# A two-layer decoder kernel: query projections in three half-width passes, and probability rings of six places

## The reference, cut to what matters

```python
x = _layernorm(x + _L0_attn_ref(x, ...))        # 16 heads of 8, causal, rope
x = _layernorm(x + _L0_xattn_ref(x, ctx, ...))  # one head of 128 over 1601 rows
x = _layernorm(x + _L0_ffn_ref(x, ...))         # 32 experts, 8 chosen, and a shared one
x = _layernorm(x + _L1_attn_ref(x, ...))        # 16 heads of 8, causal, relative positions
x = _layernorm(x + _L1_xattn_ref(x, ctx, mask, ...))  # 12 heads of 64 over 1601 rows
x = _layernorm(x + _L1_ffn_ref(x, ...))
# in _L1_xattn_ref
q = (query @ Wq.T + bq).reshape(b, tq, H, DH)
k = (cross @ Wk.T + bk).reshape(b, tc, H, DH)
scores = jnp.einsum('bqhd,bkhd->bhqk', q, k) / jnp.sqrt(jnp.float32(DH))
attn = jax.nn.softmax(where(mask, -inf, scores), axis=-1)
```

## Time and profile before

| | us |
|---|---|
| median of 3 runs | 2157.14 |
| lowest and highest of them | 2140.36, 2173.19 |
| the profiled execution's own time | 2159.29 |
| its span, first to last instruction | 2157.5 |
| TensorE busy | 1857.2 (86%) |
| GpSimd busy | 1100.0 (51%) |
| mean granted TensorE clock | 0.906 of full speed |

### The profile page before, as it was taken

The page is one execution under the profiler, slowest core; times in us unless marked ns, Lnnn a source line. Parts: engine busy times, 40 slices in busy tenths (PEclk is TensorE's granted clock), DMA queues, the critical chain, the costliest instruction groups (busy, mean ns, idle before and its releaser), DMA issues.

```text
span 2157.5 us, 50937 instructions
## 1 busy us (share of the span) xinstructions
PE 1857.2 (86%) x19672; PEld 1395.8 (65%) x19672; DVE 1189.9 (55%) x3159; ACT 903.4 (42%) x1875; POOL 1100.0 (51%) x1664
## 2 busy tenths in 40 slices
PE   5666889898898988889898988989888998989996
PEld 3443467576676666666675776756666666767775
DVE  5253447554665546744575546744477545754552
ACT  2522344444443444345343444434443453434443
POOL 2502363557535573356635674354743566356664
PEclk9975689899998998988998999988999899999998
DMA  6000010001000010000100010000000000000000
GB/s 173 26 1 1 1 26 1 1 2 27 4 2 2 2 27 4 1 3 4 27 2 2 2 27 4 2 3 2 27 4 1 2 2 4 2 1 2 2 4 3
DMA packets 24146, 23.30 MB, mean 11 GB/s; under 512 B 16266, under 2 KB 22132, under 8 KB 23412
## 3 DMA queue, kind: packets, MB, share of 16 engines
q1 hardware_dynamic: 23892, 19.89, 3.4%
HBM read 18.83 MB, written 1.05 MB: 9 GB/s over the span
## 4 chain that ended last, share of the span: by engine, by line
PE 44%; POOL 22%; issue 16%; DVE 12%; ACT 4%; POOLq 0%; SPq 0%; DMA 0%; DVEq 0%; ACTq 0%
POOL xp_l L1444 9%; POOL pr_l L1444 6%; PE ps L934 4%; PE ps L936 3%; PE ps L935 3%; PE ps L901 3%; PE ps L1112 3%; PE ps L952 3%; PE ps L953 3%; PE ps L954 3%; PE ps L896 2%; DVE smax L1730 2%; DVE xmax_x L1808 1%; PE ps L1097 1%; PE ps L1099 1%
## 5 line engine op out<-in xcount | busy, mean ns | idle before, releaser
L1444 POOL TENSOR_TENSOR xp_l<-xp 128x512 f16<-128x512 f32 (+1 forms) x672 | 665.4, 993 | 761.9 <-ACT xp L1292 754.0
L1292 ACT ACTIVATE xp<-ps 128x512 f32<-128x512 f32 (+1 forms) x672 | 380.2, 566 | 564.4 <-PE ps L936 472.1
L1808 DVE TENSOR_REDUCE xmax_x<-ps 128x1 f32<-128x512 f32 x576 | 391.9, 687 | 350.4 <-PE ps L901 342.2
L1444 POOL TENSOR_TENSOR pr_l<-pr 128x512 f16<-128x512 f32 (+1 forms) x248 | 249.5, 1030 | 131.4 <-ACT pr L1244 119.7
L952 PE MATMUL ps<-c_tok,xp 128*128 128x97 f16 (+1 forms) x1248 | 202.9, 215 | 11.5 <-POOL xp_l L1444 5.8
L952 PE MATMUL ps<-cx_tok,xp 128*128 128x97 f16 (+1 forms) x1248 | 198.1, 212 | 11.6 <-ACT oq L1302 6.1
L953 PE MATMUL ps<-c_tok,xp 128*128 128x97 f16 (+1 forms) x1248 | 201.8, 214 | 0.0
L954 PE MATMUL ps<-c_tok,xp_l 128*128 128x97 f16 (+1 forms) x1248 | 201.7, 213 | 0.0
L953 PE MATMUL ps<-cx_tok,xp 128*128 128x97 f16 (+1 forms) x1248 | 197.1, 211 | 0.0
L954 PE MATMUL ps<-cx_tok,xp_l 128*128 128x97 f16 (+1 forms) x1248 | 197.0, 211 | 0.0
L936 PE MATMUL ps<-xq_h,c_hl 96*128 96x256 f16 (+1 forms) x624 | 181.3, 291 | 0.0
(11 more groups left out here) (367 smaller groups left out, 4541.6 us busy)
## 6 DMA issues: line engine op xcount, KB each, us to landing
ct<-in_ctxT SPq DMA_DIRECT2D x8, 600.4 KB
raw_tok<-in_ctx SPq DMA_DIRECT2D x8, 576.0 KB
c_wg<-in_wg SPq DMA_DIRECT2D x1, 1088.0 KB, 7.7
c_wu<-in_wu SPq DMA_DIRECT2D x1, 1088.0 KB, 9.8
c_wd<-in_wd SPq DMA_DIRECT2D x1, 1088.0 KB, 4.9
xin<-in_x SPq DMA_DIRECT2D x8, 128.0 KB, 2.1
out<-ys SPq DMA_DIRECT2D x8, 128.0 KB, 1.9
c_wd<-in_sel SPq DMA_DIRECT2D x1, 768.0 KB
```

Of the source, the lines that this page charges most:

```text
L1292: fn(xp_slot(i, n)[0:k_, 0:w], bank(first_bank + n % 2, k_, 0, w), ACT.Exp, scale=scale).then_inc(xa_e[i].sem, 1)
L1444: sub = lambda out, a, b_: nc.gpsimd.tensor_tensor(out, a, b_, ALU.subtract)
L1808: red(cross.xmax[:, t, c:c + 1], bank(PART_BANK[q], P, 0, PARTS[c][1]), AX.X, ALU.max).then_inc(xa_xd[1].sem, 1)
```

## The change

The projection's matrices are split once at setup: `am_h` holds the high parts of `a_mat` in float16, `am_l` the low parts times 64. The tokens come as three float16 tiles in `xq_in`: high, high divided by 64, and low. `project` becomes three float16 products. ScalarE makes the first two tiles from bank 4 (two instructions where there was one copy), VectorE the third (`tokens_low`), and those who waited for `xt_ready` of stage 4 wait for VectorE's `xl_ready`. Apart from that, `pr` and `pr_l` get six places in place of four; the value products of self-attention come two pairs of chunks after their scores, in place of one pair, and those of the one-head cross-attention three pairs after, in place of two. The stream's own ring `xp` keeps its three places and its lag of two.

```diff
-STEPS = (73, 82, 206, 30, 21)
+STEPS = (75, 82, 206, 30, 21)
+RING = 6
+LOW = 64.0
-        pr = sb("pr", [P, 4, 2 * SEQ])
+        pr = sb("pr", [P, RING, 2 * SEQ])
+        am_h = sb("am_h", [P, XH, KE], F16)
+        am_l = sb("am_l", [P, XH, KE], F16)
+        xq_in = sb("xq_in", [P, 3, SEQ], F16)
-        pr_l = sb("pr_l", [P, 4, 2 * SEQ], F16)
+        pr_l = sb("pr_l", [P, RING, 2 * SEQ], F16)
...
 # TensorE, self_attention
                 for g in range(0, 12, 2):
                     scores((g, g + 1))
-                    if g:
-                        values(g - 2)
-                        values(g - 1)
-                    yield
-                values(10)
+                    if g > 2:
+                        values(g - 4)
+                        values(g - 3)
+                    yield
+                for g in range(8, 11):
+                    values(g)
                 m = values(11)
 # TensorE, context_attention
-                    if p >= 2:
-                        values(p - 2)
-                    yield
-                values(NPAIR - 2)
-                values(NPAIR - 1)
+                    if p >= 3:
+                        values(p - 3)
+                    yield
+                for p in range(NPAIR - 3, NPAIR):
+                    values(p)
 # TensorE, project
-                mm(bank(4, KE, 0, SEQ), a_mat[:, 1 + h, :], cross.xt[:, 1:1 + SEQ], start=True, stop=True, skip_group_check=True).then_inc(xa_q[1].sem, 1)
+                o = bank(4, KE, 0, SEQ)
+                mm(o, am_h[:, h, :], xq_in[:, 0, :], start=True, stop=False, skip_group_check=True)
+                mm(o, am_l[:, h, :], xq_in[:, 1, :], start=False, stop=False, skip_group_check=True)
+                mm(o, am_h[:, h, :], xq_in[:, 2, :], start=False, stop=True, skip_group_check=True).then_inc(xa_q[1].sem, 1)
 # TensorE, cross_start and step 5 of head 9
-                pe.wait_ge(xt_ready[4].sem, xt_ready[4].at(b, 1))
+                pe.wait_ge(xl_ready.sem, xl_ready.at(b, 1))
 # ScalarE, stream
+                if n == 4:
+                    nc.scalar.copy(xq_in[:, 0, :], bank(4, P, 0, SEQ))
+                    fn(xq_in[:, 1, :], bank(4, P, 0, SEQ), ACT.Copy, scale=1.0 / LOW).then_inc(xt_ready[4].sem, 1)
+                else:
+                    nc.scalar.copy(front.xt[:, 1:1 + SEQ], bank(5, P, 0, SEQ)).then_inc(xt_ready[n].sem, 1)
 # VectorE, folding, between g_mat and f_m
+                dve.wait_ge(unfolded, 2 * (1 + XH))
+                step(v.tensor_copy(am_h[:], a_mat[:, 1:, :]))
+                settle()
+                step(tt(a_mat[:, 1:, :], a_mat[:, 1:, :], am_h[:], ALU.subtract))
+                settle()
+                ts(am_l[:], a_mat[:, 1:, :], LOW, None, ALU.mult).then_inc(unfolded, 1)
 # VectorE, in cross_start and in step 5 of head 9
+            def tokens_low(b):
+                dve.wait_ge(xt_ready[4].sem, xt_ready[4].at(b, 1))
+                tt(xq_in[:, 2, :], bank(4, P, 0, SEQ), xq_in[:, 0, :], ALU.subtract).then_inc(xl_ready.sem, 1)
```

More of the change, by code:

```diff
@@ L291, in __init__ @@
             def __init__(self, c):
-                self.xt = sb("xt" + c, [P, 1 + SEQ])
+                self.xt = sb("xt" + c, [P, 1 + SEQ]) if c == "_f" else None
                 self.res = [sb(f"res{n}{c}", [P, QT, D]) for n in range(1 if c == "_f" else 2)]
@@ L388, in xp_slot @@
         def xp_slot(i, n):
-            return xp[:, n % 3, :] if i == 1 else pr[:, n % 4, :]
+            return xp[:, n % 3, :] if i == 1 else pr[:, n % RING, :]
         def pr_high(g):
-            return pr[:, g % 4, :].bitcast(BF16)[:, 1::2]
+            return pr[:, g % RING, :].bitcast(BF16)[:, 1::2]
         def xp_high(n, k_, c0, w):
@@ L441, in decoder_kernel @@
         sa_u = both("sa_u", 1)
+        xl_ready = count("xl_ready")
         sa_on = both("sa_on", 1)
@@ L655, in folding @@
                     yield
-                pe.wait_ge(unfolded, 2 * (1 + XH) + XH + 2)
+                pe.wait_ge(unfolded, 2 * (1 + XH) + XH + 3)
                 yield
@@ L795, in values @@
                             o, q0 = bank(5, P, (t * NH + h) * (HD + 1), HD + 1), k * n + (t - kt) * P
-                            high, low = pr_high(g)[:, q0:q0 + P], pr_l[:, g % 4, q0:q0 + P]
+                            high, low = pr_high(g)[:, q0:q0 + P], pr_l[:, g % RING, q0:q0 + P]
                             mm(o, high, v_h[:, kt, h, :], start=(g == 0 and k == 0 and t == 0), stop=False, skip_group_check=True)
@@ L861, in values @@
                         mm(o, c.tok_l[0:k_, kt, :], pr_high(p)[0:k_, cols], start=False, stop=False, skip_group_check=True)
-                        m = mm(o, c.tok_h[0:k_, kt, :], pr_l[0:k_, p % 4, cols], start=False, stop=(kt == NK - 1), skip_group_check=True)
+                        m = mm(o, c.tok_h[0:k_, kt, :], pr_l[0:k_, p % RING, cols], start=False, stop=(kt == NK - 1), skip_group_check=True)
                     if p == NPAIR - 1:
@@ L1040, in cross_steps @@
                                 if joins and p == 5:
-                                    pe.wait_ge(xt_ready[4].sem, xt_ready[4].at(b.plus(1), 1))
+                                    pe.wait_ge(xl_ready.sem, xl_ready.at(b.plus(1), 1))
                                 stream_part(bn, hn, q)
@@ L1183, in stream @@
                 act.wait_ge(tr_ready[n].sem, tr_ready[n].at(b, 1))
-                side, bk = (cross, 4) if n == 4 else (front, 5)
-                nc.scalar.copy(side.xt[:, 1:1 + SEQ], bank(bk, P, 0, SEQ)).then_inc(xt_ready[n].sem, 1)
+                if n == 4:
[3 more added lines that the diff above has]
+                    nc.scalar.copy(front.xt[:, 1:1 + SEQ], bank(5, P, 0, SEQ)).then_inc(xt_ready[n].sem, 1)
             def normalise(b, n, side, res):
@@ L1243, in self_attention @@
                     act.wait_ge(sa_s[i].sem, sa_s[i].at(b, g + 1))
-                    fn(pr[:, g % 4, :], bank(6 + g % 2), ACT.Exp, scale=SA_SCALE).then_inc(sa_e[i].sem, 1)
+                    fn(pr[:, g % RING, :], bank(6 + g % 2), ACT.Exp, scale=SA_SCALE).then_inc(sa_e[i].sem, 1)
                     if g % 2:
@@ L1484, in attention_low @@
                     pool.wait_ge(sa_e[i].sem, sa_e[i].at(b, g + 1))
-                    sub(pr_l[:, g % 4, :], pr[:, g % 4, :], pr_high(g)).then_inc(sa_l[i].sem, 1)
+                    sub(pr_l[:, g % RING, :], pr[:, g % RING, :], pr_high(g)).then_inc(sa_l[i].sem, 1)
                     if g % 2:
@@ L1526, in context_attention @@
                     pool.wait_ge(xa_e[0].sem, xa_e[0].at(b, p + 1))
-                    sub(pr_l[0:k_, p % 4, 0:w], pr[0:k_, p % 4, 0:w], pr_high(p)[0:k_, 0:w]).then_inc(xa_l[0].sem, 1)
+                    sub(pr_l[0:k_, p % RING, 0:w], pr[0:k_, p % RING, 0:w], pr_high(p)[0:k_, 0:w]).then_inc(xa_l[0].sem, 1)
                     yield
@@ L1876, in cross_start @@
                 residual(b)
+                tokens_low(b)
                 yield
@@ L1897, in cross_steps @@
                     for p in range(NPAIR):
+                        if h == CUT and p == 5 and not b.known(NB - 1):
+                            tokens_low(b.plus(1))
                         for ahead, q in STREAM_PARTS[p]:
```

## The result

| | before | after |
|---|---|---|
| median of 15 runs, us | 2153.78 | 2172.72 |
| lowest and highest | 2138.76, 2173.19 | 2158.11, 2191.63 |
| span of the profiled execution | 2157.5 | 2170.3 |
| mean granted TensorE clock | 0.906 | 0.874 |

What follows compares the result with a forecast made beforehand. No single limit: TensorE sets the pace where it has work, elsewhere waiting for GpSimd's low parts, with its clock another part. 43 + 21 - 4 - 3 = 57 us off 2159.3 gives 2102, written as 2103; range 2070 to 2143.

Steps and rivals of the forecast that it cites:

- the rings and the lag: In the value stages, TensorE may run further ahead of GpSimd's low parts: 43 us gained.
- the projections: 96 projections as three float16 passes, 0.27 us less each at full clock, 0.36 at half; three quarters counted: 21 us gained.
- the new wait: TensorE in step 5 waits for `tokens_low`: 0 to 0.8 us in each of 8 batches, 4 us lost.
- setup: Three dependent VectorE operations at the start delay the `f_m` copies: 0 to 5 us, 3 us lost taken.
- Rival (c): Stops at value-stage ends lower TensorE's clock, 0.39 us per us at half clock; 2214 us at 12 us each; chance 0.07.
- the one-head stages: Sign in the cross-attention's value stages: they should take about 11 us in place of 12.6.
- keep their length although these waits are gone: Sign against the prediction in the value stages: TensorE's own work at half clock would then bound them.
- Rival (d): The projection saves only one pass of 0.11 us, as waits for weights return: 8 us, not 21, so 2116; chance 0.08.
- waits at the first value product: Sign on TensorE: these waits should fall from 32 us to 15 or less, the rest at stage ends.
- stages like the one at 666.1: Sign in self-attention's value stages, 20.2 us before: about 17.5 us with GpSimd above 0.9 busy.
- waits at the stream's value products: Sign against the prediction: waits for `xp_l` at line 952 growing by more than 10 us.
- mean clock: Sign against the prediction: TensorE's mean clock moving by more than 0.01 from 0.906.

Runs made afterwards that it cites:

- e2_rings: The kernel before with only the six-place rings and the longer lags, keeping its 32-bit projection: 2134.31 us, ratio 0.9921 to the kernel before.
- e4_wait_only: The kernel before plus one unused VectorE subtraction at the place of `tokens_low`, for which TensorE waits: 2185.31 us, ratio 1.0150 to the kernel before.
- e1_projection: The changed kernel with rings of four places and the old lags, so the projection part alone: 2193.54 us, ratio 1.0191 to the kernel before.
- e5_fill_b3: The changed kernel with 16 unread products just ahead of TensorE's wait for `tokens_low` in each of seven batches: 2150.13 us, ratio 0.9961 to the kernel before.
- e10_pool_low_fill: `e8_pool_low` with four unread products more in each step of self-attention's value stages: ratio 0.9839 to the kernel before.
- e9_rings_fill: `e2_rings` with four unread products more in each step of self-attention's value stages: ratio 0.9889 to the kernel before.
- e3_early: The changed kernel with `tokens_low` earlier in VectorE's queue, ahead of the front's reductions: 2150.55 us, ratio 0.9978 to the kernel before.
- e8_pool_low: The changed kernel with ScalarE copying bank 4 in 32 bits and float16 tiles made from SBUF, the low one by GpSimd: 2148.21 us, ratio 0.9955 to the kernel before.

## Why the prediction was wrong

The sum had 43 us for the rings and the lag, 21 for the projections, -4 for the new wait and -3 for setup: 57 us faster. Against the kernel before in one set of runs, the parts measured 20 us for the rings and the lag (`e2_rings`), -31 for the wait (`e4_wait_only`), and -8 for the rest of the projection's part (`e1_projection` against `e4_wait_only`). These add up to 19 us slower, and the changed kernel measured 2172.72 - 2153.78 = 19. So three terms were off, each by 23 to 29 us.

**The new wait.** The step that failed in its mechanism is the cost of this wait, "between 0 and 0.8 us for each of 8 batches, I take 0.5, so 4 us". It measured 31 us. Two things were missed in it. I asked what stands behind `tokens_low` on VectorE, and not what it stands behind itself: "`tokens_low` ends near 966.0" is ScalarE's end plus one operation, as if VectorE were free, while the order of the pieces puts four reductions before it. That makes a wait of up to 2.0 us. And I priced a stop at its own length, when the clock behind it costs twice as much again (3.9 against 1.8 us in one stretch). Rival (c) had this mechanism and its price, 0.39 us for each us at half clock, but at another place, the ends of the value stages; the new wait was priced without it. With that price and the 10 us at half clock that the stretch shows (0.29 x 2 x 17.7), the clock's part comes to 4.0 us, where `e5_fill_b3` has 3.9. The kernel before has such stretches in two of the six batches (16.0 us at a clock of 0.68 and 14.7 at 0.77, against 12.0 at 1.00); the prediction doesn't use them.

**The rings and the lag.** The mechanism was right: TensorE's waits for low parts went from 32 to 12 us, the undisturbed stages end at 17.3 to 17.4 us with GpSimd busy nearly throughout (17.0 of 17.4), and the one-head stages take 11.7, close to the 11 forecast. The term was too large: 43 us forecast, and 0.9921, 17 to 20 us, over the whole kernel by itself. The stages gave more than that. In the trace of `e2_rings` the stretches with the self-attention's value stages took 37 us less than before (397.5 and 360.7 us) and those with the one-head stages 13 us less. But the stretches from the experts' routing to the next value stage took 19 us more (786.4 and 805.9 us), with 182 us at half clock in place of 124. The sum left that out: it priced the stages and took what lies behind them as unchanged. One trace of each kernel shows this, and no run shows why the clock is lower there; `e1_projection`, with its short lag, has as much (about 180 us), so the longer lag alone is not the cause. Three of the sixteen stages of the changed kernel were as long as before or longer (19.2 us at a clock of 0.50, 20.4 and 20.5 at 0.67 and 0.66), and two more gained only 0.7 us, at 0.66: my warning that stages might "keep their length although these waits are gone" was what happened there.

**The projection.** The saving of 0.27 us each was too much. I set three times the middle of a row of float16 passes against a whole 32-bit product that stood behind a wait. Like against like it is 0.11 us at full clock, and 0.14 behind a wait; at half clock 0.99 - 0.78 = 0.21 and not 0.36. That is one pass of 0.11 us and little more. So the count of four passes for a 32-bit product, which I took from the Trainium skill (FP8 and Floating Point Precision, TensorE Precision Notes) and set aside for the 0.60 us of the earlier trace rows, agrees with the trace: the two records take 0.22 and 0.31 us, twice two passes of 0.11 and the 0.09 at the end that the float16 row has too. Rival (d) had that size, with another cause for it. For 96 projections it is some 14 us less work, and of these 10 came out with the fill (`e10_pool_low_fill` against `e9_rings_fill`). Without it the sign turned: each kernel with the float16 projections is slower than the one nearest to it without them (`e1_projection` by 8 us, `e3_early` by 16, `e8_pool_low` by 0.3%, where the intervals of the first and the last pair overlap), and the medians of their clocks are lower, 0.875 against 0.884, and 0.885 and 0.880 against 0.895. The sum had no term for that.

**Setup.** The 3 us are not to be seen: the first two stretches of the front are not longer than before.

**The signs that I named.** The waits at the first value product fell below 15 us (12.3), the stages like the one at 666.1 came to 17.4 to 17.7 us in three of seven batches and 20.4 to 20.5 in four, the one-head stages to 11.7 in most, and the waits at the stream's value products (now line 962) grew by 4 us, from 11.2 to 15.3. A projection shows 0.15 and 0.11 us between its records after a wait. The new wait showed seven times with up to 2.0 us, and the mean clock moved by 0.032, or 0.02 like against like: more than I had called too much either way.

What stays open is why the float16 projections come with a lower clock where nothing fills the value stages. `e8_pool_low` shows the long kind of stage often; the trace of `e3_early` doesn't, but it is of an execution with an unusually high clock, and its eleven others were not traced. That the fill takes the long kind away shows only that it hangs on TensorE's work there. How the row of one column behind the projection would do ahead of it wasn't tried.

## What to carry to other kernels

Before a wait is added, read the whole queue of the engine that must answer it, from its last finished instruction to the one that answers: the cost is that queue, and not the instruction. A stop of TensorE of one or two us in a stretch that already has stops can cost three times its length by the clock behind it, so an edit that removes work or waits elsewhere can lose to one new stop; compare the granted clock of the same stretch in both profiles, and look up first whether the profiled execution has a time and a clock like those of the others. Compare prices like with like: a product behind a wait with one behind a wait, and with its edges. Where a stop can't be avoided, products that nobody reads, put exactly into it, are a cheap test of whether the clock is what is lost, and sometimes the repair.

## What the runs showed of the hardware

Stops of TensorE like the two of 1.37 and 1.71 us in the changed kernel came with 7 to 14 us at half clock in that stretch, in each of six batches, in the changed kernel, `e1_projection` and `e4_wait_only`; the same place with the second stop filled stayed at full clock in five of six (`e5_fill_b3`). A value stage had TensorE busy for 19.51 of 20.40 us and a clock of 0.67; the same work had 0.90 in another batch. A 32-bit product of 256 columns takes 0.53 us up to the start of the one-column product behind it, and 0.60 where it stands behind a wait; three float16 passes of the same size take 0.42 and 0.46. In a row of float16 passes of 256 columns one takes 0.11 us from start to start, but the last one before a product with a weight of one column takes 0.20.
